# Eight jobs between the first maximum tiles, each issued in two halves on TensorE, the first half one tile sooner

## The reference

```
x = layernorm(x + self_attention(x))        # attends over batch and head for each position, 3 iterations
x = layernorm(x + cross_attention(x, ctx))  # 16 heads of 16, keys and values from ctx: 8 x 1601 x 256
x = layernorm(x + ffn(x))                   # base matrix plus one of 8 adapters, chosen by least reconstruction loss
```

```
q = split_heads(q_in @ Wq.T)
k = split_heads(mem @ Wk.T)
v = split_heads(mem @ Wv.T)
scores = einsum('bhqd,bhkd->bhqk', q, k) / sqrt(D_HEAD)
scores = where(mem_mask, scores, -inf)
attn = softmax(scores)
out  = einsum('bhqk,bhkd->bhqd', attn, v)
```

## Time and profile before

| | us |
|---|---|
| median of 3 runs | 1708.98 (1707.59 to 1711.63) |
| profiled execution | 1710.42 |
| its span, first to last instruction | 1708.6 |
| TensorE busy (matmuls) | 1623.3 (95%) |
| VectorE busy | 1234.4 (72%) |
| ScalarE busy | 1063.1 (62%) |
| mean granted clock of TensorE | 0.991 of 2.4 GHz |

### The profile page before, as it was taken

How to read it: one execution, slowest core, us unless ns; L and a number is a source line. 1 busy time by engine, 2 the same in 40 slices (tenths; PEclk the granted TensorE clock), 3 DMA queues, 4 the chain that set the end, 5 groups by cost and what they waited for, 6 DMA issues and landing times.

```text
span 1708.6 us, 25767 instructions
## 1 busy us (share of the span) xinstructions
PE 1623.3 (95%) x9848; PEld 608.1 (36%) x9848; DVE 1234.4 (72%) x1790; ACT 1063.1 (62%) x2012; POOL 160.9 (9%) x151
## 2 busy tenths in 40 slices
PE   6869989999999999999999999999999999999987
PEld 5442323333334333333334333332334323332234
DVE  5687767877778777876778777887778777777423
ACT  2226766676666766676666666676666766666651
POOL 6310000100011000100011000100001000000000
PEclk9889999999999999999999999999999999999999
DMA  5654070714315070624307070533506050410000
GB/s 153 118 143 85 25 136 15 113 38 102 60 46 104 24 132 21 105 59 87 75 24 122 18 136 26 94 69 76 86 1 138 25 85 26 87 26 2 4 25 16
DMA packets 101342, 116.58 MB, mean 68 GB/s; under 512 B 21834, under 2 KB 86987, under 8 KB 101220
## 3 DMA queue, kind: packets, MB, share of 16 engines
q1 hardware_dynamic: 98484, 113.89, 33.2%
q10 hardware_dynamic: 2736, 1.06, 0.3%
HBM read 80.12 MB, written 34.78 MB: 67 GB/s over the span
## 4 chain that ended last, share of the span: by engine, by line
PE 84%; ACT 5%; DVE 5%; issue 4%; DMA 1%; ACTq 1%; SPq 0%; POOL 0%; POOLq 0%; DVEq 0%
PE banks L1107 22%; PE values L1126 22%; PE banks L1081 12%; PE work L990 5%; PE work L1004 5%; ACT xprobs L1256 4%; PE work L947 4%; PE work L1017 3%; PE work L1011 3%; PE work L932 3%; DVE xneg_max_pieces L1444 1%; PE work L1020 1%; PE work L996 1%; PE work L1029 1%; DVE xv_rows L1402 1%
## 5 line engine op out<-in xcount | busy, mean ns | idle before, releaser
L1256 ACT ACTIVATE xprobs<-banks 128x512 f32<-128x512 f32 x1664 | 902.4, 595 | 451.0 <-PE banks L1107 436.2
L1444 DVE TENSOR_REDUCE xneg_max_pieces<-banks 128x2 f32<-128x1024 f32 x768 | 910.2, 1220 | 279.6 <-PE banks L1081 277.4
L1107 PE MATMUL banks<-xq_stacks,xk_stacks 99*128 99x512 bf16 (+1 forms) x1664 | 523.1, 385 | 28.0 <-ACT xprobs L1256 20.1
L1126 PE MATMUL values<-xprobs,xv_rows 128*17 128x512 f32 x3328 | 437.9, 598 | 1.0 <-ACT xprobs L1256 1.0
L1107 PEld LDWEIGHTS banks<-xq_stacks,xk_stacks 99*128 99x128 bf16 (+1 forms) x1664 | 128.1, 97 | 418.6 <-ACT xprobs L1256 278.5
L1081 PE MATMUL banks<-xk_stacks,xq_stacks 49*128 49x512 bf16 (+1 forms) x2048 | 249.3, 336 | 9.1 <-DVE xneg_max_pieces L1444 8.2
L1081 PEld LDWEIGHTS banks<-xk_stacks,xq_stacks 49*128 49x128 bf16 x2048 | 56.5, 94 | 280.1 <-DVE xneg_max_pieces L1444 160.5
L1511 POOL TENSOR_TENSOR xk_parts<-xk_rest,xk_parts 128x401 bf16<-128x401 f32 (+1 forms) x64 | 59.0, 922 | 712.3 <-ACT xk_parts L1217 712.3
L1126 PEld LDWEIGHTS values<-xprobs,xv_rows 128*17 128x17 f32 x3328 | 55.1, 95 | 120.6 <-issue 119.1
L1506 POOL TENSOR_TENSOR xrstd<-xrstd,mhalf 128x4 f32<-128x4 f32 x23 | 23.2, 1010 | 649.8 <-DVE xrstd L1316 649.8
L1004 PE MATMUL work<-xvT,ctxT_a 128*128 128x128 f32 (+1 forms) x416 | 57.1, 282 | 3.1 <-DVE xk_rest L1377 1.9
(11 more groups left out here) (301 smaller groups left out, 1063.7 us busy)
## 6 DMA issues: line engine op xcount, KB each, us to landing
xk_stacks<-key_parts_dram SPq DMA_DIRECT2D x186, 200.1 KB, 11.5
key_parts_dram<-xk_parts SPq DMA_DIRECT2D x144, 100.0 KB, 1.7
xq_stacks<-parts_dram SPq DMA_DIRECT2D x186, 64.0 KB, 8.0
ctxT_a<-in_ctxT SPq DMA_DIRECT2D x4, 1601.0 KB, 7.3
ctxT_b<-in_ctxT SPq DMA_DIRECT2D x4, 1601.0 KB, 7.6
parts_dram<-xq_parts SPq DMA_DIRECT2D x45, 128.0 KB, 1.9
key_parts_dram<-xk_parts SPq DMA_DIRECT2D x48, 100.2 KB, 2.9
xa<-in_x SPq DMA_DIRECT2D x8, 512.0 KB, 13.8
```

The source lines that it names most:

```text
L1107: pe.matmul(scores[n % SRING], kst[0:ROWS[par], k, h2, par, t * P:(t + 1) * P], qst[0:ROWS[par], k, h2, par, :], start=True, stop=True).th ...
L1126: last = pe.matmul(av[32 * j:32 * j + HD + 1, :], vals[:, k, t, gr * GH + j, :], probs[:, sl % 2, j, :], start=t == 0, stop=t == XKT - 1)
L1256: nc.scalar.activation(probs[:, sl % 2, j, :], scores[n % SRING], ACT.Exp).then_inc(exped, 1)
L1444: nc.vector.tensor_reduce(nmp[:, of % 2, j2, :, q, piece], pairs[n % MRING][:, :, :], AX.X, ALU.max, negate=True).then_inc(on["mxr"], 1)
```

## The change

The job that stood before tile n is issued in two parts: part 0 before tile n-1 (with its wait for the bank and, for a `v` job, for the loaded weights), part 1 before tile n. It holds for the eight jobs before tiles 5 to 24; the first halves stand before tiles 4, 7, 10, 13, 16, 19, 21 and 23. A `kproj` or `qproj` half is one contraction step of two, a `v` half is two of its four 128-key tiles. Jobs at n > 26 stay whole. The programs of the other engines are as before.

```diff
                 if n == N_REST:
                     pe.wait_ge(stacked_head, 16 * 2 * TOP)
-                if n in BETWEEN_TILES:
-                    if BETWEEN_TILES[n][0] == "v":
+                split = n < MXG and n + 1 in BETWEEN_TILES
+                if split:
+                    if BETWEEN_TILES[n + 1][0] == "v":
                         pe.wait_ge(loaded, N_LOADS)
-                    pe_job(FIRST, BETWEEN_TILES[n])
+                    pe_job(FIRST, BETWEEN_TILES[n + 1], 0, 2)
+                elif n in BETWEEN_TILES:
+                    if n > MXG:
+                        pe_job(FIRST, BETWEEN_TILES[n])
+                    else:
+                        pe_job(FIRST, BETWEEN_TILES[n], 1, 2)
                 pe_pair(of, x, n)
```

## The result

| | before | after |
|---|---|---|
| median of 19 runs each, us | 1710.10 (1707.56 to 1715.04) | 1719.48 (1712.95 to 1727.54) |
| ratio, 95% interval | | 1.0047 [1.0035, 1.0058] |
| profiled execution / its span, us | 1710.42 / 1708.6 | 1715.95 / 1714.2 |
| mean granted clock, profiled execution | 0.991 | 0.986 |
| mean granted clock, mean over the runs | 0.990 (35 runs) | 0.985 (19 runs) |

The change costs 8 us by the ratio, 6 to 10 by its interval. I had forecast +1.8, put 1714 at the top of the range and given 0.75 to a difference that can't be told from none: wrong in size, and the loss is clear of noise. The profiled execution after is one of the quicker ones, 5.5 us above the one before; the half of the runs above 1719.5 is not seen in it.

What follows compares the result with a forecast made beforehand. Bound before the main loop: a chain through the single work bank, whose release starts each job. Tiles +1.40 and clock +0.4 on the profiled 1710.42 gave 1712.2, as median 1708.98 + 1.8 = 1710.8 us; range 1707.5 to 1714.

Steps and rivals of the forecast that it cites:

- The direction of the mechanism: At the single work bank: its release sets a job's start; each early half puts one more tile behind it; +1.40 us.
- kproj 4 and its tiles: Tiles 4 and 5, low clock: tile 4's 0.43 us, once hidden in TensorE's idle, enters the path; +0.44 us.
- kproj 5: Tiles 7 and 8: tile partly in the path before, more of the job under the high clock; +0.02 us.
- The tiles: Eight split jobs ahead of the main loop: sum of their costs without the clock, +1.40 us.
- a tile's is 0.22: At v 4 and v 5, high clock: the tile between the halves adds 0.22 us to each.
- Kproj 6 and 7: 0: Tiles 14 and 20 are ready some 0.7 us sooner, but VectorE reads four tiles without a pause; 0 us.
- I take 0, as TensorE is still busy from 82.39 without a pause: First clock rise, at 85.2 during kproj 5: unchanged, 0 us taken, with bounds of -1.42 to +1.7.
- The low clock stays: Rival: the rise at 85.2 is missed, v 4 and the rest of kproj 5 run low; 1713.6 to 1714, chance 0.16.
- The clock swings: Rival, inside 86 to 111 us: one low stretch costs +1.46, two 2.9; 1711.8 to 1713.3 us, chance 0.05.
- The rule that I cited: For TensorE: small idle times between matmul groups cycling through banks can make the clock swing; the change would lose.
- Is the delay kept: Behind the last maximum tile the chain is unbroken, so all 1.40 us is kept; 0 if some cover existed.
- this place of the clock: Clock rise near 119.4, around v 0 and v 1 after the store: +0.4 us taken, bounds -1.46 to +1.46.

Runs made afterwards that it cites:

- the pauses were filled: The changed kernel plus idle matmuls into an unused bank ahead of the waits before tiles 4, 7, 10, 16 and 21; 1710.9 us, 1.0009 to the kernel before.
- the second half later: Against the kernel before, seven jobs have their second half before tile n+1, and VectorE reads a kproj one tile later; 1718.5 us, ratio 1.0044.

## Why the prediction was wrong

**The direction of the mechanism was right.** VectorE idles 2.35 us before tile 4 (2.3 forecast) and not before tile 5 (0.3 forecast), and the first halves start at the releases I named. That two sums agree with the profile is luck: kproj 4 and its tiles cost +0.49 from VectorE's read of the qproj head to tile 5 (before 76.07 to 80.13, after 73.16 to 77.71; forecast +0.44), kproj 5 +0.05 (5.39 to 5.44; forecast +0.02), but with a clock that rose at 77 and fell at 80.4, where I had it low until 85.2. Where it stays low, in the kernel with only kproj 4 and 5 split, the first of these stretches takes 4.90 us against 4.06: +0.84.

```profile
76.79 0.28 DVE L1391 SCALAR_TENSOR_TENSOR xq_rest<-work,xq_parts 128x128 f32<-128x128 f32 x1
...
81.69 1.23 DVE L1444 TENSOR_REDUCE xneg_max_pieces<-banks 128x2 f32<-128x1024 f32 x1 [0.46 <-PE banks L1081]
```

**The tiles were sized at 1.40 us and cost 3.06** at the high clock. The term "a tile's is 0.22" was too small: two halves of v 5 with a tile between span 2.47 us to the tile behind (95.43 to 97.90), against 1.96 for the whole job. That is 0.51 for the tile, of which 0.29 goes to the breaks. At the low level half and tile of kproj 4 took 1.64 and 0.53 us (73.50, 75.14, 75.67) where I had 1.49 and 0.43. And at the high clock kproj 4 costs 1.08: VectorE's read of tile 4 and the memset, which I had placed under the job, run without a pause up to tile 5 (76.64 to 78.49) and are now the path. "Kproj 6 and 7: 0" was near: -0.18 each.

**The step that failed is the clock,** "I take 0, as TensorE is still busy from 82.39 without a pause". I had priced the rise at 85.2 alone. In the profiled execution the clock rose early, then fell at 80.4, behind the pause before kproj 5, which had grown from 0.99 to 1.69 us, and stayed low to 90.6, so that v 4 ran low as in my rival "The low clock stays" (0.16): 2.05 and 2.08 us for its halves against 2.02 for the whole. And it fell at 104.3, my rival "The clock swings" (0.05). Both together I had not priced. From tile 8 to tile 11 the path took 7.04 us against 4.24 (+2.80, forecast +0.22), and from tile 17 to the maxima 15.01 against 12.96 (+2.05, forecast +0.50). Of the 5.73 us lost from the qproj head's read to the maxima (34.46 against 40.19), these two hold 4.85. The evidence that I used against it was that the clock stayed at 1.00 through idle times of 1 us. But the change doesn't keep these: it puts the tile behind the wait, so the 0.93 and 0.18 us around tile 16 become 1.31 in one piece, and the 1.59 us before v 6 become 2.38. I had written down that the pause before kproj 5 grows and did not carry this to the other places.

Over all runs the mean clock is lower by 0.005. At the 1.0 to 1.2 us that 0.001 goes with in these runs (last section) that is 5 to 6 us, and with 3 us of path it makes the 8: an estimate from their spread, not a sum read in a trace. The rule that I cited (the Trainium skill, TensorE: Matmul & The Clock Gate, A second HAM failure mode: psum-queue depth-cycling) is borne out: the clock swung inside the stretch, and the loss beyond the path was gone when the pauses were filled.

**"Is the delay kept"** held only in part. The changed kernel was 2.82 us behind at the maxima and 3.66 at the loop's first kproj (forecast for this place of the clock: +0.4). Then the low stretch from 126.5 to 129 did not come again, the kproj took half as long, and group 0 was 1.97 behind. In one execution that is luck:

```profile
126.36 2.66 PE work L990 x4
...
130.02 1.35 PE work L990 x4
```

In the loop the delay grew by 3.4 us up to group 2, where the load of the maxima came late and the clock fell behind it. The same happened in one other of the profiles, that of the second half later, at 228 to 236 us. Whether the change makes it likelier stays open: the low stretch there was seen in 2 of 13 profiles, the two with the longest fronts (45.8 us).

**The forecast of the spread** was too narrow. One profiled execution gives one pattern of low stretches. 35 runs of the kernel before range over 0.987 to 0.994 in mean clock and over 12 us (1704.06 to 1716.02), the 29 of a later series over 0.983 to 0.993 and 16 us (up to 1721.11), the 19 of the changed kernel over 0.982 to 0.990 and 15 us.

## What to carry to other kernels

Before moving a wait ahead of other work on TensorE, write down TensorE's pauses before and after: the same idle in one piece can cost more than the work that is moved. Where two kernels differ in the granted clock, compare them also with the pauses filled, which separates the path from the clock, and look where the low stretches lie, as some have nothing to do with the edit. Filling alone (16 matmuls that nobody reads) gave more here than either way of splitting the jobs. No split here paid: only kproj 6 and 7 could start earlier, and nobody waited for them. Ask first who frees the bank.

## What the runs showed of the hardware

The granted clock of one and the same kernel differs from execution to execution, and the time goes with it: over the 19 runs of the changed kernel by 1.2 us for each 0.001 of mean clock (correlation -0.71), over three series of the kernel before by 1.0 (35 runs, -0.64), 1.35 (29 runs, -0.88) and 0.7 us (23 runs, -0.48). The length of a pause alone doesn't tell whether the clock falls behind it: with only the wait moved it fell behind pauses of 1.41 and 1.81 us and not behind one of 1.50 in the same execution, and in the kernel before it did not fall behind 1.59. Breaking a float32 group of 16 in two with another group between cost 0.29 us beyond that group's own 0.22.
